# A wait for the preceding block's rows ahead of each block of gathers, in the edge stage of a graph transformer layer

## What is computed

```
xn = _layernorm(x, axis=-1)
# graph attention, with a loop edge per node
h = (xn @ W).reshape(n, H, F)
a_src = jnp.sum(h * att_src[None], axis=-1)
a_dst = jnp.sum(h * att_dst[None], axis=-1)
e = jax.nn.leaky_relu(a_src[src] + a_dst[dst], 0.2)
m = jax.ops.segment_max(e, dst, num_segments=n)
ex = jnp.exp(e - m[dst])
denom = jax.ops.segment_sum(ex, dst, num_segments=n)
alpha = ex / (denom[dst] + 1e-16)
msg = h[src] * alpha[..., None]
out = jax.ops.segment_sum(msg, dst, num_segments=n)
# linear attention over xn, then
x = x + gnn(xn) + mix(xn)
x = x + ffn(_layernorm(x))
```

## Time and profile before

| | us |
|---|---|
| median of three timed runs | 3565.35 (3564.39 to 3574.77) |
| profiled execution, span from first to last instruction (its only time on record) | 4403.2 |
| GpSimd busy in the profile | 2160.0 (49%) |
| VectorE busy | 2365.2 (54%) |
| TensorE busy | 3041.5 (69%) |

### The profile page before, as it was taken

How to read it: one execution, slowest core, us unless ns; L and a number is a source line. 1 busy time by engine, 2 the same in 40 slices (tenths; PEclk the granted TensorE clock), 3 DMA queues, 4 the chain that set the end, 5 groups by cost and what they waited for, 6 DMA issues and landing times. The chain is left out here.

```text
span 4403.2 us, 70224 instructions
## 1 busy us (share of the span) xinstructions
PE 3041.5 (69%) x17326; PEld 2470.3 (56%) x17327; DVE 2365.2 (54%) x6486; ACT 1275.7 (29%) x4257; POOL 2160.0 (49%) x2117
## 2 busy tenths in 40 slices
PE   6566666666676776666666777676323349999998
PEld 5444545545555554455555555555323349999997
DVE  7544444444444444545555555555788865555554
ACT  6422222222222222222222222222455523333332
POOL 3255555555555555444444544444066644444444
PEclk9778777878888887878888888888555559999999
DMA  7544444444444444444444444444455724444443
GB/s 262 173 117 117 111 115 112 119 108 111 109 119 111 115 114 117 121 126 121 128 126 122 133 126 125 126 120 111 127 169 186 238 96 71 72 70 72 70 71 55
DMA packets 384652, 529.69 MB, mean 120 GB/s; under 512 B 64276, under 2 KB 323559, under 8 KB 384218
## 3 DMA queue, kind: packets, MB, share of 16 engines
q0 software_dynamic: 114496, 265.49, 25.5%
q1 hardware_dynamic: 185112, 183.84, 14.8%
q10 hardware_dynamic: 84770, 77.19, 5.5%
HBM read 394.80 MB, written 132.72 MB: 120 GB/s over the span
## 5 line engine op out<-in xcount | busy, mean ns | idle before, releaser
L1133 POOL DMA_INDIRECT rows<-node_rows,index x1552 | 1480.9, 954 | 1392.6 <-SPq L1102 930.3
L1411 PE MATMUL ps_sum<-msg,hot 128*128 128x260 f32 x3904 | 1220.7, 465 | 40.0 <-issue 27.9
L1411 PEld LDWEIGHTS ps_sum<-msg,hot 128*128 128x128 f32 x3904 | 853.5, 230 | 198.4 <-issue 45.3
L1391 PE MATMUL ps_hot<-ident_h,hotT 128*128 128x128 bf16 x1952 | 223.5, 247 | 729.7 <-ACT hot L1293 338.6
L1391 PEld LDWEIGHTS ps_hot<-ident_h,hotT 128*128 128x128 bf16 x1952 | 154.3, 110 | 832.8 <-issue 549.4
L1213 DVE TENSOR_TENSOR msg<-rows,ps_w 128x1024 f32<-128x1024 f32 x488 | 596.1, 1222 | 45.1 <-ACT ps_w L1305 29.1
L2140 POOL DMA_INDIRECT out_dram<-big x204 | 352.7, 1729 | 438.3 <-DVE big L2232 390.9
L1195 DVE TENSOR_REDUCE e<-ps_tgt 128x32 f32<-128x96 f32 x488 | 123.3, 253 | 801.2 <-remote 728.2
L1293 ACT ACTIVATE hot<-ps_hot 128x512 f32<-128x512 bf16 x488 | 290.2, 595 | 736.3 <-remote 589.0
L2166 PEld LDWEIGHTS x_ps_hT<-x_rowsT,x_w_now 128*128 128x128 f32 x3264 | 398.0, 192 | 11.5 <-DVE x_w_now L2210 1.1
L2166 PE MATMUL x_ps_hT<-x_rowsT,x_w_now 128*128 128x128 f32 x3264 | 399.1, 276 | 0.7 <-DVE x_w_now L2210 0.7
(11 more groups left out here) (289 smaller groups left out, 4194.9 us busy)
## 6 DMA issues: line engine op xcount, KB each, us to landing
targets<-dst_row SPq DMA_DIRECT2D x391, 128.0 KB
big<-expert_in SPq DMA_DIRECT2D x204, 130.0 KB
rows<-node_rows,index POOLq DMA_INDIRECT x1564
node_rows<-big SPq DMA_DIRECT2D x14, 924.0 KB
turned<-rT SPq DMA_DIRECT2D x14, 896.0 KB, 4.6
area<-turned ACTq DMA_DIRECT2D x98, 128.0 KB
queries<-area ACTq DMA_DIRECT2D x98, 128.0 KB
area<-queries ACTq DMA_DIRECT2D x98, 128.0 KB
```

The lines of the kernel that those rows point to most:

```text
L1133: g.indirect_dma_start(rows[:, j, k, :], None, s.node_rows, bass.IndirectOffsetOnAxis(ap=index[:, b, j * G + k:j * G + k + 1], axis=0)).th ...
L1391: mm = pe.transpose(ps_hot[:, k * P:(k + 1) * P], hotT[:, j % 2, k * P:(k + 1) * P], ident_h[:, :])
L1411: mm = pe.matmul(ps_sum[:, j % 2, 0:SUM], hot[:, j % MSGS, k * P:(k + 1) * P], msg[:, j % MSGS, k, :], start=(k == 0), stop=(k == G - 1))
```

## The change

In `gather`, for each block after the fourth (q above EARLY), GpSimd waits, ahead of the first of the four gathers and behind the wait for the slot, until all four gathers of the block before have landed. The awaited value is 64 for each time that the slot of the block before has been filled.

```
--- before.py
+++ after.py
@@ -1128,6 +1128,10 @@
                         g.sem_inc(s.wait_seen, 1)
                     if not isinstance(q, int) or q >= RING:
                         g.wait_ge(slot_free, q - (RING - 1))
+                        g.sem_inc(s.wait_seen, 1)
+                    if not isinstance(q, int) or q > EARLY:
+                        landed = two_turns * (2 * 16 * G) + ((m - 1) // RING + 1) * (16 * G)
+                        g.wait_ge(rows_in[(m - 1) % RING], landed)
                         g.sem_inc(s.wait_seen, 1)
                     for k in range(G):
                         g.indirect_dma_start(rows[:, j, k, :], None, s.node_rows,
```

## The result

The changed kernel takes **4525.74 us** in the median of four runs (4525.43 to 4532.58), the kernel before 3568.21 us (3564.39 to 3574.77): a ratio of 1.2689, interval 1.2671 to 1.2707, slower by 957 us. The prediction had the direction and the bound, and a time of 4120 us in a range up to 4240 us: the size was wrong by 406 us.

What follows compares the result with a forecast made beforehand. GpSimd's successive gathers were taken to bound the timed edge stage; 388 blocks of 6.72 us, 2607 us against 2035, add 572 us, giving 4138 us, lowered to 4120 us for the extra hop; range 3880 to 4240 us.

Steps and rivals of the forecast that it cites:

- What bounds the kernel: Edge stage: timed runs are GpSimd issuing gathers one after another, 2034.6 us; the profiled execution waits for slow consumers.
- The sum against the profiled execution's own span: Edge stage: a 2607 us chain of gathers is less than the profiled execution's 2872.4 us, so no loss.
- The change's instructions at nothing: Ahead of each block's first gather: added wait, increment and register instructions cost nothing, running in the 0.30 us gap.
- The block after the change: Chain of gathers: three issue steps, 3.76 us, plus the fourth gather's landing, 2.96 us, make 6.72 us a block.
- the extra hop: Landing rows include a hop over SyncE to VectorE that the new wait lacks, so each is an upper bound.
- the two rows: At the edge stage's start, fourth gather's issue to VectorE's one-hot: 3.33 us for block 3, 2.96 us for block 4.
- the sum of 4138 us: Whole run: timed chain of 2035 us grows to 388 x 6.72 = 2607 us, +572 us, giving 4138 us.
- the ends: Chain of gathers: landings of 2.5 and 3.33 us give 6.26 and 7.09 us a block, 3960 and 4282 us.
- The estimate from that page: Chain of gathers: a landing of 2.3 us by the skill page, 6.07 us a block, some 3885 us.
- No change: Edge stage: consumers at 7.40 us a block hide the 6.72 us chain behind six slots; 3565 us, chance 0.06.
- faster: Edge stage: pauses after blocks let TensorE's held-back signals through early; 3300 us, chance 0.04.
- slower by little: Edge stage: timed gathers without the 0.30 us gap, 5.35 us a block; +41, 3606 us, chance 0.10.

Runs made afterwards that it cites:

- the small operation: The changed kernel with a small memset on GpSimd between the added wait and each block's first gather: 4590.34 us, ratio 1.2871.

## Why the prediction was wrong

**What bounds the kernel**: right. That 838 us of the profiled span were not in a timed run's edge stage, and that a timed run is GpSimd's gathers one after another, came out as worked out: 2041.7 us of chain against 2034.6, and less time once GpSimd has fewer gathers. The sum against the profiled execution's own span, by which nothing would be lost, was of no use, as that execution was not like the others.

**The change's instructions at nothing**: right; the wait for the block two before carries them all and costs nothing.

**The block after the change**: wrong. The step "After, it costs three issue steps and then the time from the fourth gather's issue to its landing: the next block may start only then" left out a term, and the sentence that the extra hop makes each row of landing an upper bound hid it. Those rows end at the start of a VectorE instruction. A gather that the same landing releases starts 0.60 us later than that. By this view the time from issue to the next start is 3.93 us, 0.60 of lag and 3.33 of landing as VectorE would see it. The mean landing thus came out at the upper of the two rows, 3.33, where the lower was taken; single blocks run from 2.9 to 4.9. With less than 20 KB of other transfers beside the awaited gather, as above (223 of the 310 blocks), VectorE sees it after 3.16 us, else after 3.70, so a single pair of rows could not give the mean. The terms: lag 0.60, landing 0.37 above the value taken, together 0.97 of the 1.02 us by which 7.74 us exceeds 6.72; 388 times that is 376 of the 388 us between 4525.74 and the sum of 4138 us. Taking 18 us off the sum for the hop was a step in the wrong direction.

The lag could have been read before. SyncE issues its next transfer right behind the count that frees a slot, and in the trace of before it does so at

```profile
871.76 0.33 SPq L1084 DMA_DIRECT2D targets<-dst_row  x1
```

while the released gather of the earlier trace rows starts at 872.48, 0.72 us later; over the 166 such releases of that trace it is 0.73 us at the median, and never less than 0.71. Part of it may have stood in the earlier trace rows already, if the small operation is read as above: each gather has 0.30 us of idle time ahead of it, and the sum counted three of these gaps a block and none ahead of the released gather. With 0.72 us added, the ends would have been 6.98 and 7.81 us a block, 4239 and 4561 us, with the measured time between them.

The Trainium skill, "DMA: Bandwidth & Descriptors", section "Anatomy of one DMA — SWDGE (gpsimd) path", puts the sequencer's dispatch at about 50 ns and, by its fit, a gather of this size at 2.3 us. The runs show a lag of 0.60 us and a landing of 2.7 us at the least and 3.3 us at the median. The estimate from that page was 3885 us, farther off still.

**The rivals.** No change, faster, and slower by little are all out: the profile of before whose time is that of the timed runs holds none of the stalls that the first two needed, and its gathers follow in 1.25 us steps, which the third needed shorter. Of the signs named for the profile after, the fours of gathers came; 1.7 us of idle time ahead of each first gather was 2.98, and 6.5 to 7 us a block was 7.74.

## What to carry to other kernels

A wait for one's own transfer costs the landing and then the start of the next one, and the start isn't hidden any more once the engine stands: read the second where an engine was released by anything, not only the first. Waiting for an event one block older, or three issue steps later, kept almost all of the time here. A landing is also not one number: what the awaited landing sets off elsewhere runs beside the next gathers, and the one that is awaited should be read at its own place. And where a profiled span and the timed runs differ by a quarter, first settle which of the two a stage's rows describe.

## What was not expected of the hardware

An indirect DMA on a GpSimd that stood starts 0.60 us after VectorE takes up work on the same landing, block after block, while a memset there starts at 0.12 us; behind another gather the gap is 0.30 us. A landing isn't fixed either: it goes with the other transfers in flight. The second gather behind a release, which meets SyncE's and ScalarE's transfers, ends 3.4 to 3.5 us after its issue; the awaited ones that meet little of them end after 2.6 us, whether none, one or two gathers are issued behind them.
